# The same instructions in another order: all five engine orders and the ring of PSUM banks of a macaron layer laid out anew

## The reference

```python
x = x + 0.5 * ffn(layernorm(x))      # front
x = x + attention(layernorm(x))
x = x + 0.5 * ffn(layernorm(x))      # back
```

## Time and profile before

| | |
|---|---|
| median of 3 runs | 498.22 us (498.04 to 498.91) |
| profiled execution, its own time | 501.7 us |
| its span, first to last instruction | 499.9 us |
| mean granted clock of TensorE | 0.963 |
| busy share of the span | PE 89%, PEld 48%, DVE 82%, ACT 66%, POOL 60% |
| chain that ended last | PE 60%, DVE 17%, POOL 7%, ACT 6%, issue 5%, DMA 2% |

### The profile page before, as it was taken

How to read it: one execution, slowest core, us unless ns; L and a number is a source line. 1 busy time by engine, 2 the same in 40 slices (tenths; PEclk the granted TensorE clock), 3 DMA queues, 4 the chain that set the end, 5 groups by cost and what they waited for, 6 DMA issues and landing times.

```text
span 499.9 us, 10127 instructions
## 1 busy us (share of the span) xinstructions
PE 444.7 (89%) x3294; PEld 241.2 (48%) x3294; DVE 411.4 (82%) x1320; ACT 331.0 (66%) x748; POOL 301.2 (60%) x323
## 2 busy tenths in 40 slices
...
DMA packets 21124, 14.52 MB, mean 29 GB/s; under 512 B 2952, under 2 KB 20944, under 8 KB 21072
## 3 DMA queue, kind: packets, MB, share of 16 engines
...
## 4 chain that ended last, share of the span: by engine, by line
PE 60%; DVE 17%; POOL 7%; ACT 6%; issue 5%; DMA 2%; SPq 1%; POOLq 0%; ACTq 0%; DVEq 0%
PE bank L1209 10%; PE bank L1254 10%; PE bank L1232 10%; PE bank L1259 4%; PE bank L1162 4%; PE bank L1163 3%; PE bank L1164 3%; PE bank L1276 3%; DVE bank L894 3%; DVE m_part L963 2%; DVE diff L857 2%; PE bank L1180 2%; POOL sums L620 2%; PE bank L1134 2%; ACT scaled L705 2%
## 5 line engine op out<-in xcount | busy, mean ns | idle before, releaser
L740 ACT ACTIVATE prob<-bank,exp_scale 128x512 f32<-128x512 f32 x288 | 189.1, 691 | 68.0 <-PE bank L1237 42.2
L620 POOL TENSOR_TENSOR sums<-sums,prob 128x1024 f32<-128x1024 f32 x48 | 112.7, 2367 | 0.7 <-ACT prob L740 0.7
L1209 PE MATMUL bank<-k_stack,q_stack 96*128 96x512 f16 (+3 forms) x384 | 102.8, 332 | 7.8 <-DVE m_fin L959 4.6
L1232 PE MATMUL bank<-q_stack,k_stack 98*128 98x512 f16 (+3 forms) x384 | 104.3, 331 | 3.3 <-ACT prob L740 2.1
L705 ACT ACTIVATE scaled<-bank,gate 128x128 f32<-128x128 f32 x256 | 80.3, 374 | 28.1 <-POOL x L598 14.4
L591 POOL TENSOR_TENSOR pair_sum<-dve_sum,scaled 128x256 f32<-128x256 f32 x64 | 46.8, 731 | 86.4 <-DVE dve_sum L943 76.7
L963 DVE TENSOR_REDUCE m_part<-bank 128x1 f32<-128x512 f32 x128 | 82.9, 678 | 4.3 <-PE bank L1209 4.2
L959 DVE CUSTOM_DVE_ANT_0 masked<-bank,mask_qk 128x384 f32<-128x384 f32 (+1 forms) x128 | 76.1, 612 | 6.1 <-PE bank L1209 5.8
L1254 PE MATMUL bank<-prob,v_lat 128*32 128x512 f32 (+3 forms) x768 | 79.0, 496 | 0.0
L1162 PE MATMUL bank<-we_hi,xT_hi 128*128 128x512 f32 x128 | 65.8, 514 | 0.9 <-ACT scaled L705 0.6
L1232 PEld LDWEIGHTS bank<-q_stack,k_stack 98*128 98x128 f16 x384 | 34.0, 99 | 58.1 <-ACT prob L740 27.3
...
## 6 DMA issues: line engine op xcount, KB each, us to landing
...
```

What stands on the lines that cost most here:

```text
L620: nc.gpsimd.tensor_tensor(into, first if j == 1 else into, new, ALU.add).then_inc(sum_step, 1)
L740: nc.scalar.activation(prob[:, n % NP, :], bank[ST + n % NST][:], ACT.Exp, scale=exp_scale[:, 0:1]).then_inc(p_ready, 1)
L1209: last = mm(into[:, n * w:(n + 1) * w], q_stack[0:MROW, c, g * NR + r, (i % TC) * P:(i % TC + 1) * P], k_stack[0:MROW, b % 2, g, k:k + w], ...
L1232: last = mm(into[:, at:at + CH - off], k_stack[:, b % 2, g, j * P:(j + 1) * P], q_stack[:, c, g * NR + r, off:CH], start=at == 0, stop=not ...
```

## The change

All five strings are replaced. Each holds the same letters as before in the same numbers (PE 942 steps of 538 with a bank, DVE 1180, ACT 744, POOL 308, SP 116), so every engine executes the same instructions as before, and only their order, the banks of the ring, and the waits that follow from these differ. On average a step moves by 2.7 places on PE, 4.4 on DVE, 2.3 on ACT, 0.9 on POOL and 1.2 on SP. 130 of the 538 uses of the ring keep their bank. Nothing outside the strings is changed. The first line and the last of each string, as the diff has them (those between are replaced in the same way):

```diff
 PE_ORDER = steps(
-    "PX6PL7Y2Y3Y6X5PL5Y7Y2Y3Y6PY7Y2Y3Y6Y7Y5Y1Y2Y3UUx6Q7K5W0X1x2Q3Q6M7M5M1M2K3M7X0M5W6L1M2M6LM3M7M0M5M2Y6Y3M7Y0M5R"
...
-    "Y7SSVY1SSVSY5SVSSY7SSSVSVSY0SSY1SV7VVY5Y2Y3Y0J7JJJY6Y1Y5z2l3Y7Y0Y6Y1Y2Y5Y3Y7"
+    "X6L7Y2PPY3Y6X5L5PY7Y2Y3Y6Y7Y2Y3Y6PY7Y5UY2Y3Y6x1UQ7K5X2W3Q6x0Q1M7M5M2X0M6M3M7L5LM2K0W1M6M1Y3M7Y0Q2M6M1M7R6M1M"
...
+    "1SSVSSz5SSY7SSSVSSY5Sl0SVSSVSV6VVY1Y2Y3Y7J6JJJY5Y0Y1Y2Y3z6l7Y0Y5Y1Y6Y3Y2Y7Y0"
 )
 DVE_ORDER = (
-    "XXXXNNNNNNNXXXXNNXXNXNXXXNXNXNIHGGGGGGNGGGGGGNGGGGGGNGGIGNGGGGNGNGGNGCGCGGCGCGGCGCGGGCGCGGCGCGCGGCGCGxGGCGGC"
-    "GCGxCPCCCxxnnnnnnnCPCCCCPCPCxPCPxCCCCXxXXXxnnnnnnPnQXKXXXNNIQMMQMMKMIMMGGGNGGMGMGMGMGMGGGNGNGMGMGGGMGRGNGMGG"
...
-    "CGGGGCGCGGGCGGGGGGCCCGCDDGDGCCCCCCCCJzzzzmmmmmmmCCCCCiCCCGGGGGGGGGGGGGGGGGGGGGGGGGGGCCCCCCCCCCCCCCCC"
+    "XXXXNNNNNNNXXXXNHINNNNNGGGNGGGGGGGGGGGGGXGXGXGXGXXXGXINGGNGGNGNGGNGNGNGGCGCGCGCGCGGGCGCGCGGxGCGCGCCGGCGGGGCC"
+    "GCGPxCCCCxxPnnnnCnnnCCCCXCCPPCxXCXxCCCPXPxxnnnnnnnPQKIXXXXNNQMMMIQMGGGGGNGNGMGNGMGGGKGMGMGMGMGMGMGRGMGMGGGGQ"
...
+    "GGGCGGGGGGGCCGGGDGDGDGCCGCGCCCCCJzzzzmmmmmmmCCCCCCCCCCiCCGGGGGGGGGGGGGGGGGGGGGGGGGGGCCCCCCCCCCCCCCCC"
 )
 ACT_ORDER = (
-    "NNNNHXNNPNNLPXCCCCCCCPCLCCCCCCPCCCCPCCCCCCCCCCnnnnCCCCxNQNNNKXnnnnxNQNNNQWKWXLRQCCCCCECECCCECCCERECCECCECCEC"
...
-    "CCEmCmmmCCOEECCzCCCECEEEEECEEECCEECEEECECECEEEECElCECCCEEOCCCCCCCCCCCCmmmmCCCzClCCCCCCCCCCCCCCCC"
+    "NNNNHXLPPNNNNXCCCLCCCCCPCCPCCCCCCCCCCCCCCPCCCCnnCCCnCnxNNQNNKnnnnXxNQNNNWQXLKWQRCCCCCCCEECEECECCCECCECCECCCC"
...
+    "CRCCCCCOEECCEECCCEEECmECEmEEmmEEEEzEECECECECEEEECCElECOCCCCCCCCCCCCCCCmmmmCCzlCCCCCCCCCCCCCCCCCC"
 )
 POOL_ORDER = (
-    "NNNNNFFFFFFFFFNFFFFFFnnFFFFFFFFFnnFFFFFFFFFFFFNFFFnnNYFFFFFFYFAAFAFAAAAnnAAAAAAAFFFFFAAYFYFFFFFFYmmNFFFYnnAF"
...
-    "AFFAFAAAFFYAAYFFFmmYFAAAYAAAFFAFmFmAFFFFFYFFFFFFAAAAFAFAFAAFFFFFYFFFFFFFmmFFFFFFFFFFFFFFFFFF"
+    "NNNNNFFFFFNFFFFFFFFFFnFnFFFFFFFFnnFFFFFFFFFFFFnFnNFFFNFFYFFFYFAFAAFAAAAnnAAAAAAFAAFAFFFFYFFYFNmmFYFFFFYFAnFN"
...
+    "AFFAFAAAAAFFYFYFFmmFYAAAYAAAFFFAFFAFFmFmFYFFFFAAAFAFAAAAFFFFFYFFFFFFFmmFFFFFFFFFFFFFFFFFFFFF"
 )
 SP_ORDER = (
-    "LLQQQKKKKQQKQQKQRRQQQRLRQRRKQQKQLQQKRRQQKRQKRKQQRQQRRRQQQKKKRQRQQRKRKQKQOQQRQQRRRKQQQKKQQRQRQQRKQKKRQQORQRRR"
-    "ORROOOOO"
+    "LLQQQKKKQQQRQKRQKKQQRQRQLRRKQQKQLQQKQRRQKKQQRRKQQRQRRRKKKQQQQQQRRRRKKQKOQQQQRQRRRQQKQQQKKROQRQKQKQRKRQQRORQR"
+    "RORROOOO"
 )
```

More of the change, by code:

```diff
@@ L195 @@
-    "Y7SM6SM0Q5Y1Y6M0K7Y1SSQ0Y6M5SM7SVM5M7M1SSY0Y6M5R7SM1VSSM5M7Y6SM1SM5M0M7SVVSM1SM5M0M6SM7SM1SM5Y0M6SSM7M1M5SM6"
-    "SVV7SM1SM5M0M6SR1VVSM5SM0M6M7SM1W5SSM0M6M7M1SM0SV6SM7M5M1SM0SJ7JJJR5SM1M0SSVVVM7SSM1M0M5SM6SM7SM1V0SM5SM6z7M"
-    "1SM5SM6VVSM1M5Sz6SM7M1SVl5lSM7SY6SM1M7SVVVSSJ0Y1SSM7JJJSSM7Y5Y0SSVVSSM6Y1Y7SSR0Y6SV5VVSSY0z7SY1SY5l6SSSSY0SS"
-    "Y7SSVY1SSVSY5SVSSY7SSSVSVSY0SSY1SV7VVY5Y2Y3Y0J7JJJY6Y1Y5z2l3Y7Y0Y6Y1Y2Y5Y3Y7"
+    "X6L7Y2PPY3Y6X5L5PY7Y2Y3Y6Y7Y2Y3Y6PY7Y5UY2Y3Y6x1UQ7K5X2W3Q6x0Q1M7M5M2X0M6M3M7L5LM2K0W1M6M1Y3M7Y0Q2M6M1M7R6M1M"
@@ new lines @@
+    "6Y7M1M2M6Y5M1SSY6M0SSM7Y1SSM0Y5Y7M6SSM0Y1Y6M0M5SM7SR0M1Y5M7M0V1Y7M5M0SSM6VSM5M0M7M6VVM5SM0SM7x6M5SM0SM1M6M7V"
+    "5M0SM1M6SM7VM0SM1R6M7VVY0Y6M1SSM7Y5Y1SM0M7SK6Q5M0SM7SM1M0SQ7M6SSM5VVSM1SM7M0M6SJ5JM1SSM7JJM0SSM6M1M7M5SM0SVV"
+    "M6SM1SX7M5M0SSVM6SSM1M5W0R6SSM0V1VVSM5M6Sx0M7M1SM5M6M0SSK7VM1SSQ5X6M0SSM7W1R0SL6LSY7M0SSM5VVSSQ1SY0SSM5VSSM6"
+    "Y1SSM5Y6M7M0SSVM5SM7M1SR0M5SM7SM1Y0SM5M7SV1VVSM5SM7M6SM1M5M7SM6SM0Y1SM5SV7VVVSM6M0M1M5SM7SM6Y0M1SSJ5JSM7SM6J"
+    "JY1SR7SM0M6V5VY7SM0M6VVSM1SY0M6SM5SY1Y6SVY7M5M0Sz1M6SM5SY0z6SJ5Jl1lVM6SSM7M0JJY6M7SSx5M0VY7SM5SK0M6SSM5VSM0S"
@@ new lines @@
+    "Q6W5SM7M0SQ5SM6M7SM0VY6M7SSM0M1V7VVR0M6Y1X5M7M6Y0Y1Y7SSM5M0Y1SM6Y5x0SM7Y6Y0SM1SY7M5M6SK1Y5M6M0SVY6R7M0SX1M5S"
+    "M0SQ7M5SL0LY1M5SM7SQ6Y5SM7SVVY7M1SSM6W5Y1SSM6M7Y5SSM6VVY1R7M0SSM6Y5Y1SM0Y6SM7SM1Y5SSM0Y7M1SM6SM0Y5Y1SSM6M7Y0"
+    "SM5SM6M7M1V5VVM6SM7Y1SM0SM5Y6SSM7J0JJJY5M1M6SSM0Y7M1SM6V0VVVY5M1SM6M0Y7SR1SV6VM0SSM1x5M7Sz0M1VVM7SSM1z5Q6K0l"
+    "7lSSM5J6JSM1SJJSSM0M5Q1SM0SVVVM6SSM5x0M1SY6SM5SW1SSM5Y0Y7M1M5SM0SM6Y1SM5Y0M6M7SM5VY6M7SM1SR5VV7VVY0M1M5SSM6Y"
+    "7SM1M5SY6M1SM0SQ5Y1M6M7SK0Y6SSY7M5M1SY0SM5SM1Q6Y5SR7M1SVVM7SSM0M6Y1SM7SVM0SM6SM5M7M0SM6SM5SVVM7SM0M6SM1SM5R7"
```

30 lines of the change are left out of this document (16 added, 14 removed).

## The result

The changed kernel takes 482.77 us (median of 4 runs, 481.98 to 487.51), the kernel before 498.57 us beside it; the ratio is 0.9692, 95% interval 0.962 to 0.9765: 15.4 us faster (11.7 to 18.9). The forecast was 496.0 us, with a range from 490.0 to 501.8. The sign was right, the size was off by a factor of seven. Some executions of a kernel run longer at a lower granted clock; the ratios compare only the others.

The account below looks back on a forecast made before the run. PE was taken as the bound, with only its 55.2 us of idle and the clock movable. Terms +0.9 - 1.1 - 1.4 + 0 - 0.6 = -2.2 us took the median 498.22 to 496.0 us, range 490.0 to 501.8.

Parts of the forecast that it names:

- All other stops and ring waits: Mainly the middle, 80 to 440 us: waits redrawn with no net gain, between 3 us earlier and 3 later.
- head and first S: Start of the kernel: head up to the first M block 0.9 us later, first scores S 1.1 us earlier.
- the stop at 128 us: Layernorm step of chunk 3 on DVE, 5.04 us long beside POOL's sums: 1.4 us earlier (6.4 earlier to 1.5 later).
- the end: After 440 us, up to the last join: 0.6 us earlier, between 1.65 earlier and 1.0 later.
- the first S: First scores, at 74.02 us before: 1.1 us earlier through fewer DVE reductions ahead, between 2.0 and 0.
- x 0: Transposes of the first chunk on PE, at 40.12 us before: 1.4 us later, at 41 to 42 us.
- rival (c): Slower by the head: first chunk's transposes 2.1 us late, projections 1.5 us longer; +3.0 us, 501.2 us; chance 0.25.
- the one tile: At the end, one ffn tile less ahead of POOL's last sum, 1.65 us.
- The gate: At the end, twelve gate steps of chunk 6 on DVE, some 3.4 us, ahead of the last quad's denominators.
- Rival (d): No effect: PE is the bound for 360 us, stages reached earlier just wait; 498.2 us; chance 0.15.
- (a): Whole early start kept: head ends 3.0 us earlier instead of 0.9 later, -3.9, 492.1 us; chance 0.10.
- (b): Long DVE stop at 128 us goes altogether with its clock loss: -6.4 instead of -1.4, 491.0 us; chance 0.10.

Follow-up runs that it names:

- The splice: New order on all engines up to 90 us, order of the kernel before behind it: 495.68 us, ratio 0.9942.
- the old order without stops: Kernel before, its order kept, small DVE steps given one SBUF input (layernorm mean and variance, router bias left out): 483.89 us, ratio 0.9678.
- The splice with the new tail: Order of the kernel before up to 435 us, changed order only behind it: 496.15 us, ratio 0.9948.

## Why the prediction was wrong

The failed step is the one that reads "All other stops and ring waits are drawn anew [...] I count **nothing** for all this, between 3 earlier and 3 later, a quarter of the 12.1 us of idle each way". In its place the runs showed one mechanism: small DVE steps held inside POOL's instructions, 20.8 us of it before and 8.4 after, which is worth some 10 of the 15.4 us. To place the terms I compare the times at which PE starts the same place of its string in the two profiled executions (new minus old): -2.5 us at step 180, -7.8 at step 220, -16.3 at step 860, -19.4 at the last.

| term | forecast | profiled executions |
|---|---|---|
| head and first S (+0.9 - 1.1) | -0.2 | -2.5 |
| the stop at 128 us | -1.4 | -5.3 |
| all other stops and ring waits | 0 (-3 to +3) | -8.5 |
| the end | -0.6 | -3.1 |
| sum | -2.2 | -19.4 |

In the medians the sum is -15.8 (498.57 to 482.77): the profiled execution of before was a late one, mostly at 128 us as shown, so that term is nearer to -2.9 there. The sign of the forecast owes little to its reasons: the head and the first S were forecast at -0.2 from two terms of either sign, and the largest gain came from the term put at nothing.

**The head.** Three readings were right in kind: the router starts at 14.02 (forecast 14 to 15), the first S is earlier, and x 0 is later. But x 0 starts at 42.90, past 41 to 42 and past the 42 from which rival (c) was to decide, and (c) did not come: the delay was swallowed by 71 us. The first S is at 71.47 against 74.02, 2.55 us earlier instead of 0.2, and ahead of the forecast 72.5 to 74.5. The place is the wait of 3.61 us for the reductions at 64.56; the longest wait for m_fin from 60 to 80 us is now 0.4 us. I had charged the 12 instead of 15 reductions ahead of R at half. The splice prices it at 2.9 us (1.8 to 4.0); how this divides over the single edits of the head was not tried.

**The stop at 128 us.** The stop went as I put it: the step is short (0.31 us), the merge behind it now waits one sum out (2.41 us, PE idle 0.85), and no stretch is below a clock of 0.8 between 130 and 145 us (1.00 from 134.4 to 143.0, against 0.60). The way there was not the forecast one. The step was to begin near 126.6; it began at 123.57, by luck 0.29 us before the end of a sum, and step 2 and the merge behind it were held in its stead. The size was read from a single execution, as if 5.04 us were this order's property.

**The other stops.** Here the reasoning failed, not only the size. I had the rows: 16 small steps of over 0.36 us (the trace has 17, three of them tensor_scalar with one input, so that not each held step has both inputs in SBUF), their ends at POOL's boundaries, PE waiting behind them. I then asked whether the new strings have fewer dependent steps or shorter runs of sums (they don't), and concluded that the draws would be equal. What counts is how many steps start inside a sum and how much of the sum is left, and on that I had no estimate: the steps held fell from 19 to 12, those of them inside a sum from 14 to 8, and the held time from 20.8 to 8.4 us. I took the 12.1 us of idle for the whole stake and a quarter of it for the most that could move. The stake was the idle time plus the time at a lower clock, and nearly all of it was this one mechanism, as the old order without stops shows (1.2 us idle in 345, clock 1.00). The new order got 8.9 of the 12.1 us; PE's idle time in the middle is 3.2 us, where 8 to 13 were forecast. The sum of DVE's excess over the undisturbed length of such steps would have told this stake before any run; the prediction counted the steps and did not add them up. That the stops can fall so much was open to me; that they would could hardly be told from the strings, and a range that reached down to 482 was what the rows allowed.

**The end.** From the last join to the end it is 28.8 us (480.5 - 451.68), forecast 28 to 29. The last sum of POOL ends at 447.24, 19.56 us earlier than the 466.80 of before; 16.3 of these came with PE's lead. The forecast 1.5 to 3.5 had some 1.6 of lead in it, so the end's own 3.3 is twice the 1.65 of the one tile that I allowed for. The gate, which I had eating this gain, was not in the way: the denominators' transpose at 448.42 waited 0.81 us for PE and not for gate steps. The splice with the new tail gives 2.6 us (1.4 to 3.7), against a forecast of 0.6 and a bound of 1.65. In its trace the last sum ends at 462.15, 4.65 us earlier than before, of which 3.1 are PE's lead ahead of the seam: about 1.5 is the tail's own, near the 1.65 of the tile. What more the end gained in the changed kernel was not tried.

Rival (d), a bound PE that lets nothing through, was wrong for the same reason as the forecast of the middle. Rivals (a) and (b) had 3.9 and 6.4 us in single places; each place did give 2 to 3 us in the medians, and the bulk was spread between them.
